# Attention with top-4 expert routing on one core: transposes and logits set between the products of a step, and ScalarE's evacuations in another order

## The chip, the cores and the metric

The kernel runs on one core of a Trainium2 chip. The metric is the device time of one execution in microseconds (us), from which the profile shows the span between the first and the last instruction. The engines are TensorE (PE; its weight loads are listed as PEld), VectorE (DVE), ScalarE (ACT), GpSimd (POOL) and SyncE (SP), which issues most transfers.

## The reference

`x` is 4 batches of 1024 rows of 1024; the context is 4 x 1024 x 512. Cut to what matters:

```python
def xattn(teacher_logits, teacher_features, Wq, bq, Wk, bk):
    query = einsum('bnc,dc->bnd', teacher_features, Wq) + bq
    key = einsum('bnc,dc->bnd', teacher_features, Wk) + bk
    attention = softmax(einsum('bnd,bmd->bnm', query, key), axis=-1)
    return einsum('bln,bmn->blm', teacher_logits, attention)

x = x + xattn(layernorm(x), ctx, Wq, bq, Wk, bk)
x = x + ffn(layernorm(x), ...)   # 32 experts, top 4 per row, SwiGLU with limits
```

The ffn computes logits of each row against `gate_w` (32 x 1024), takes the four largest, weighs them by a softmax, and sends each row through its four experts. In the attention the rows of LN1(x) are multiplied by the transposed attention matrix, so both operands have to be transposed to stand with the contracted index on the partitions.

## The kernel before

The kernel has two parts. The first, `attention_and_routing`, computes the attention, the second layernorm (LN2), the routing and a table of the rows for the experts. The second, `experts`, goes through 32 experts and is not touched. The order in each part is written out by hand: every engine has its own program, and semaphores tie them.

A batch has 8 tiles (NT) of 128 rows. A step `s` works on two batches at once: for batch `b1` it makes tile `s` of the attention matrix (energies, exponent, probabilities, transposes) and of the LN1 rows; for batch `b2`, whose attention matrix is complete, it computes the product of tile `s` and its LN2, and, one tile late (`late`, tile `n = s - 1`), transposes the LN2 rows, computes their logits, ranks and destinations. `schedule` runs the first batch alone, then a hardware loop of three rounds, whose body is steps 2 to 7 of one pair of batches and steps 0 and 1 of the next, and then the last batch's products alone. The steps with `s >= 2` and both batches are 18: six in each of three rounds. In the first two rounds, steps 2 to 5 (`CTX_STEPS`) also transpose a quarter of the next context, and step 7 is followed by the projections `queries_and_keys` of the next batch.

An f32 value is kept as two f16 words, high (HI) and low (LO), so a product of 128 x 1024 x 1024 is three passes (`PASSES`) over 8 blocks and two halves of columns: 48 matmuls of 512 columns into `psM` (line 622). Transposes move 8 blocks of 128 x 128 as 32-bit words into one PSUM tile, `psT` (line 587 for rows and probabilities, line 596 for context). `psT` is shared: LN1 rows (`xnh`), probabilities (`ah`), LN2 rows (`xs2`, shown as `xs`) and context (`cx`, shown as `W`) all pass through it, and each has to be evacuated by ScalarE before the next may enter. The logits are 8 matmuls of 32 columns (line 677), the energies two of 512 (line 581), the rank of a tile two small ones (lines 708, 709).

ScalarE in a step: exponent (500), evacuation of the probabilities (505), high part of the LN2 rows (534), high parts of probabilities and LN1 rows (509, 511), evacuation of the LN2 rows (541), of the context (486), of the LN1 rows (515), exponent of the top four logits (550). VectorE in a step: maximum of the energies (762), LN1, scale, low part of the LN2 rows (786), destinations, low parts of probabilities (774) and LN1 rows (777), top four, then the read of the products (839) and LN2 (732 to 737).

Of the kernel before, what the change touches and what calls it, by code (L numbers as in the profile page):

```python
# [6 lines left out]
ACT = mybir.ActivationFunctionType  # L7
# [6 lines left out]
P = 128  # L14
# [40 lines left out]
def guarded(eng, cond, body):  # L55

    if cond is None:
        body()
    else:
        with eng.If(cond):  # L60
            body()
# [68 lines left out]
def attention_and_routing(nc, g):  # L130
# [8 lines left out]
    with ExitStack() as ctx:  # L139
# [153 lines left out]
        def following(bk):  # L293
            return bk[0], bk[1] + 1

        def per(n, bk, offset):

            return bk[0] * n + (bk[1] * n + offset)

        def tile(bk, offset):  # L300
            return per(NT, bk, offset)
# [174 lines left out]
        def _(act):  # L476
# [17 lines left out]
            def step(s, b1, b2, more):  # L494
# [18 lines left out]
                def rows_out(s):  # L513
                    act.wait_ge(s_xT, tile(b1, s + 1))
                    act.activation(XT_w[:, :, s * P:(s + 1) * P], psT[:, :].rearrange("p (k q) -> p k q", q=P),
                                   ACT.Copy).then_inc(s_xTev, 1)

                if b1 is not None:
                    guarded(act, own, exponent)
                    if s >= 1 and b2 is not None:  # L520
                        guarded(act, own, lambda: attention_out(b1, s - 1))
                    elif s >= 1:

                        if s - 1 in CTX_STEPS:
                            context(following(b1), s - 1 - CTX_STEPS[0])
                        rows_out(s - 1)
# [37 lines left out]
        def _(pe):  # L564
# [14 lines left out]
            def energies(m):  # L579
# [2 lines left out]
                                   qk[:, 1, h * HALF:(h + 1) * HALF], start=True, stop=True)  # L582
                op.then_inc(s_E, 1)

            def transpose_words(src, done):
                for k in range(KH):
                    op = pe.transpose(psT[:, k * P:(k + 1) * P], src[:, k * P:(k + 1) * P], ident[:])
                op.then_inc(done, 1)

            def context(bk, pair):  # L590

# [23 lines left out]
                    context((0, 0), pair)  # L615
                queries_and_keys((0, 0))

            def product(out, bk, t, h, blocks):

                for k in blocks:  # L620
                    for n, (a, c) in enumerate(PASSES):
                        op = pe.matmul(out[:, h * HALF:(h + 1) * HALF], XT[:, k, t * P:(t + 1) * P, a],  # L622
                                       AT[:, par(bk), c, k, h * HALF:(h + 1) * HALF].rearrange("p o q -> p (o q)"),
                                       start=k == 0 and n == 0, stop=k == KH - 1 and n == 2)
                return op

            def step(s, b1, b2, more):
                own = more if s < 2 else None
                late = lagged(b2, s, 1)

                def next_energies():
                    if s < NT - 1:
                        pe.wait_ge(s_exp, tile(b1, s + 1))
                        energies(s + 1)

                if b1 is not None and b2 is None:

                    next_energies()

                if b1 is not None and s >= 1:  # L640
                    def attention_in():
                        alone(pe, s_xTev, tile(b1, s), s_past)
                        pe.wait_ge(s_alo, tile(b1, s))
                        transpose_words(ah_w[(s - 1) % 2], s_AT)
                    guarded(pe, own, attention_in)
                if b2 is not None and s == 0:
                    alone(pe, s_xTev, tile(b2, NT), s_past)
                    pe.wait_ge(s_alo, tile(b2, NT))
                    transpose_words(ah_w[(NT - 1) % 2], s_AT)
                if b2 is not None and s < NT:  # L650

                    if b1 is None and s > 2:
                        pe.wait_ge(s_exp, B * NT)
                        pe.wait_ge(s_x2, tile(b2, s - 1))
                    elif s > 0 or not first(b2):
                        pe.wait_ge(s_x2, tile(b2, s))
                    if s == 0:

                        pe.wait_ge(s_ATev, tile(b2, NT - 1))
                    product(product_of(s, b1), b2, s, 0, range(KH))  # L660
                if b2 is not None and s == 0:
                    alone(pe, s_ATev, tile(b2, NT), s_past)
                if late:
                    bt, n = late
                    if b1 is not None and s >= 1:
                        guarded(pe, own, lambda: alone(pe, s_ATev, tile(b1, s), s_past))
                    pe.wait_ge(s_xs2, tile(bt, n + 1))
                    transpose_words(xs2, s_x2T)
                if b2 is not None and s < NT:
                    product(product_of(s, b1), b2, s, 1, range(KH // 2))  # L670
                if late:

                    pe.wait_ge(s_x2Tev, tile(bt, n + 1))
                    if n >= 1 or not first(bt):
                        pe.wait_ge(s_lgev, tile(bt, n))
                    for k in range(KH):
                        op = pe.matmul(psR[:, 0:E], x2T[:, k, :], gateT[:, k, :], start=k == 0, stop=k == KH - 1)
                    op.then_inc(s_lgt, 1)
                if b1 is not None:
                    if b2 is None and s >= 1:  # L680
                        pe.wait_ge(s_ATev, tile(b1, s))
                    if s in CTX_STEPS:
                        guarded(pe, more, lambda: context(following(b1), s - CTX_STEPS[0]))
                if b2 is not None and s < NT:
                    product(product_of(s, b1), b2, s, 1, range(KH // 2, KH)).then_inc(s_xm, 1)
                if b1 is not None:
                    if s in CTX_STEPS:
                        guarded(pe, more, lambda: alone(pe, s_cTev, per(NT // 2, following(b1), s - CTX_STEPS[0] + 1), s_past))

                    def rows_in():  # L690
                        pe.wait_ge(s_xlo, tile(b1, s + 1))
                        transpose_words(xnh_w, s_xT)
                        if b2 is not None:
                            next_energies()
                    guarded(pe, own, rows_in)
                    if s == NT - 1:
                        def next_batch():

                            alone(pe, s_exp, tile(b1, NT), s_past)
                            if b2 is not None:  # L700
                                alone(pe, s_x2, tile(b2, NT), s_past)
                            queries_and_keys(following(b1))
                        guarded(pe, more, next_batch)
                if late:

                    pe.wait_ge(s_mask, tile(bt, n + 1))
                    pe.wait_ge(s_seen, tile(bt, n + 1))
                    pe.matmul(psQ[:, 0:E], before[:], mask[:, n % 2, :], start=True, stop=False)
                    pe.matmul(psQ[:, 0:E], ones[:], seen[:], start=False, stop=True).then_inc(s_rank, 1)

            schedule(pe, step, prepare)

# [537 lines left out]
```

## Time and profile before

| | |
|---|---|
| time, median of 3 runs | 3249.12 us (3247.87 to 3255.22) |
| profiled execution: time, span | 3258.53 us, 3256.7 us |
| mean granted clock of TensorE | 0.974 |
| PE busy | 3115.6 us (96%) |
| DVE busy | 1721.5 us (53%) |
| ACT busy | 1289.4 us (40%) |
| POOL busy | 592.3 us (18%) |

### The profile page before, as it was taken

The page shows a single profiled execution, that of the slowest core. Times are in us where ns is not written, and L with a number is a line of the kernel's source. Part 1 is how long each engine was busy: PE and PEld are TensorE (multiplying, and loading weights), DVE is VectorE, ACT ScalarE, POOL GpSimd, SP SyncE. Part 2 cuts the span into 40 slices and gives each one's busy share as a digit, 9 for nine tenths or more (in the row PEclk, how much of TensorE's full clock was granted, in tenths as well). Part 3 has the DMA queues.
Part 4 walks back from the last instruction along what each step waited for, and adds up shares of the span by engine and source line. Part 5 has one row for each costly group of instructions (what it writes and reads, how often), then busy time and mean ns, then how long its engine had stood idle before and what let it go on. Part 6 is the DMA issues. An engine that isn't in the chain of part 4 may idle for free.

```text
span 3256.7 us, 46843 instructions
## 1 busy us (share of the span) xinstructions
PE 3115.6 (96%) x15456; PEld 1610.8 (49%) x15457; DVE 1721.5 (53%) x2851; ACT 1289.4 (40%) x1299; POOL 592.3 (18%) x502
## 2 busy tenths in 40 slices
PE   6799999995999999999999999999999999999997
PEld 3455555553454554454554454554444554545553
DVE  3576767764554444555444546454455444554432
ACT  3444434422343343444433434353344433443421
POOL 0022333322111111111111111111111111111111
PEclk8899999997999999999999999999999999999998
DMA  4123222244555555566655656665566655555432
GB/s 150 65 104 111 98 104 98 98 161 138 148 166 139 155 148 155 172 172 168 191 148 155 174 142 195 191 174 155 146 171 168 192 148 155 153 163 143 116 59 58
DMA packets 210440, 468.03 MB, mean 144 GB/s; under 512 B 57762, under 2 KB 57762, under 8 KB 210115
## 3 DMA queue, kind: packets, MB, share of 16 engines
q0 software_dynamic: 45856, 152.33, 20.9%
q10 hardware_dynamic: 94576, 225.46, 20.7%
q1 hardware_dynamic: 69938, 89.38, 8.3%
q8 instruction: 36, 0.59, 0.1%
q14 instruction: 34, 0.27, 0.0%
HBM read 354.64 MB, written 112.46 MB: 143 GB/s over the span
## 4 chain that ended last, share of the span: by engine, by line
PE 74%; DMA 1%; issue 0%; ACT 0%; DVE 0%; SPq 0%; POOL 0%; POOLq 0%
PE psG L1166 23%; PE psU L1166 23%; PE psY L1188 23%; PE psX L1172 4%; PE psA L1179 2%; DMA acc<-y,idxs 0%; DMA idxs<-slots 0%; DMA idxg<-slots 0%; DMA xg<-xn_tab,idxg 0%; DVE y L1113 0%; ACT y L1047 0%; ACT xT L1036 0%; SPq L962 0%; POOL acc L1004 0%; SPq L963 0%
## 5 line engine op out<-in xcount | busy, mean ns | idle before, releaser
L1166 PE MATMUL psG<-W,xT 128*128 128x512 f16 x3456 | 771.4, 380 | 2.8 <-ACT xT L1036 2.8
L1188 PE MATMUL psY<-W,aT 128*128 128x512 f16 x3456 | 769.4, 379 | 1.7 <-ACT aT L1040 1.7
L1166 PE MATMUL psU<-W,xT 128*128 128x512 f16 x3456 | 769.4, 379 | 0.0
L1166 PEld LDWEIGHTS psG<-W,xT 128*128 128x128 f16 x3456 | 338.5, 98 | 412.1 <-issue 4.7
L1188 PEld LDWEIGHTS psY<-W,aT 128*128 128x128 f16 x3456 | 338.0, 98 | 377.3 <-ACT aT L1040 1.9
L1166 PEld LDWEIGHTS psU<-W,xT 128*128 128x128 f16 x3456 | 338.2, 98 | 375.6
L123 DVE SCALAR_TENSOR_TENSOR W<-stage,W 128x2048 f16<-128x2048 f32 x192 | 438.5, 2284 | 3.8 <-ACT W L118 3.8
L1113 DVE SCALAR_TENSOR_TENSOR y<-bias,idxs,y 128x1024 f32<-128x1024 f32 x144 | 184.9, 1284 | 456.2 <-ACT y L1047 456.2
L1004 POOL DMA_INDIRECT acc<-y,idxs x144 | 226.3, 1571 | 986.3 <-DVE y L1113 970.9
L118 ACT ACTIVATE W<-stage 128x2048 f16<-128x2048 f32 x192 | 365.8, 1905 | 48.7 <-issue 38.0
L1047 ACT ACTIVATE y<-psY,idxs 128x1024 f32<-128x1024 f32 x144 | 160.3, 1113 | 515.8 <-DMA idxs<-slots 498.9
L999 POOL DMA_INDIRECT xg<-xn_tab,idxg x146 | 155.2, 1063 | 1094.3 <-PE psX L1172 663.3
L622 PE MATMUL psM<-W,XT 128*128 (+1 forms) x1392 | 333.4, 395 | 2.0 <-DVE xr L839 2.0
L1036 ACT ACTIVATE xT<-psX 128x1024 f32<-128x1024 f32 x145 | 148.6, 1025 | 449.4 <-PE psX L1172 449.4
L1121 DVE SCALAR_TENSOR_TENSOR gt<-psG,bias 128x512 f32<-128x512 f32 x144 | 99.5, 691 | 387.6 <-PE psG L1166 367.0
L1083 ACT ACTIVATE sg<-gt 128x512 f32<-128x512 f32 x144 | 91.0, 632 | 454.8 <-DVE gt L1124 454.5
L1132 DVE SCALAR_TENSOR_TENSOR up<-psU,bias 128x512 f32<-128x512 f32 x144 | 99.5, 691 | 304.5 <-PE psU L1166 304.5
L622 PEld LDWEIGHTS psM<-W,XT 128*128 128x128 f16 x1392 | 141.4, 103 | 161.4 <-issue 24.3
L465 POOL DMA_INDIRECT slots<-pack,dest x128 | 169.4, 1324 | 228.7 <-DVE tok L814 197.6
L1172 PE MATMUL psX<-ident,xg 128*128 128x128 f32 x1160 | 151.3, 274 | 20.8 <-DMA xg<-xn_tab,idxg 20.8
L1172 PEld LDWEIGHTS psX<-ident,xg 128*128 128x128 f32 x1160 | 136.5, 142 | 49.4 <-DMA xg<-xn_tab,idxg 21.7
L1142 DVE SCALAR_TENSOR_TENSOR ahl<-av,ahl 128x512 f16<-128x512 f32 x144 | 105.4, 732 | 43.1 <-ACT ahl L1089 39.7
(136 smaller groups left out, 2309.8 us busy)
## 6 DMA issues: line engine op xcount, KB each, us to landing
stage<-in_L_ffn_w_down ACTq DMA_DIRECT2D x62, 1024.0 KB
stage<-in_L_ffn_w_up ACTq DMA_DIRECT2D x61, 1024.0 KB
stage<-in_L_ffn_w_gate ACTq DMA_DIRECT2D x60, 1024.0 KB
stage<-in_x SPq DMA_DIRECT2D x32, 512.0 KB
xr<-in_x SPq DMA_DIRECT2D x32, 512.0 KB
acc<-xr SPq DMA_DIRECT2D x32, 512.0 KB
xn_tab<-x2h SPq DMA_DIRECT2D x32, 512.0 KB
bias<-in_L_ffn_b_down ACTq DMA_DIRECT2D x32, 512.0 KB
```

Of the source, the lines that this page charges most:

```text
L118: act.activation(W[:, par, HI, c * CHUNK:(c + 1) * CHUNK], stage[:, c % RING, :], ACT.Copy, scale=S_W).then_inc(s_whi, 1)
L123: dve.scalar_tensor_tensor(out=W[:, par, LO, c * CHUNK:(c + 1) * CHUNK], in0=stage[:, c % RING, :], scalar=S_W, in1=W[:, par, HI, c * CHUN ...
L465: pool.indirect_dma_start(out=slots[:, :], out_offset=bass.IndirectOffsetOnAxis(dest[:, n % 2, k:k + 1], 0), in_=pack[:, n % 2, k, :], in_ ...
L622: op = pe.matmul(out[:, h * HALF:(h + 1) * HALF], XT[:, k, t * P:(t + 1) * P, a], AT[:, par(bk), c, k, h * HALF:(h + 1) * HALF].rearrange( ...
L999: pool.indirect_dma_start(out=xg[:], out_offset=None, in_=xn_tab[:, :], in_offset=bass.IndirectOffsetOnAxis(idxg[:, 0:1].bitcast(U32), 0)) ...
L1004: pool.indirect_dma_start(out=acc[:, :], out_offset=bass.IndirectOffsetOnAxis(idxs[:, 0:1].bitcast(U32), 0), in_=y[:], in_offset=None, com ...
L1036: act.activation(xT[:].rearrange("p k q a -> p (k q a)").bitcast(F32), psX[:], ACT.Copy).then_inc(s_xTev, 1)
L1047: act.activation(y[:], psY[:], ACT.Copy, scale=idxs[:, 2:3].bitcast(F32)).then_inc(s_y0, 1)
L1113: dve.scalar_tensor_tensor(out=y[:], in0=bias[:, par, 2 * I:], scalar=idxs[:, 1:2].bitcast(F32), in1=y[:], op0=ALU.mult, op1=ALU.add).then ...
L1166: op = pe.matmul(ps[:], xT[:, k, :, a], weights(par, c, offset + k * I, I), start=k == 0 and n == 0, stop=k == KH - 1 and n == 2)
L1172: op = pe.transpose(psX[:, n * P:(n + 1) * P], xg_w[:, n * P:(n + 1) * P], ident[:])
L1188: op = pe.matmul(psY[:, h * HALF:(h + 1) * HALF], aT[:, k, :, a], weights(par, c, 2 * KH * I + k * H + h * HALF, HALF), start=k == 0 and n ...
```

## The change

For the 18 steps with both batches and `s >= 2`, TensorE runs a new function `both` and ScalarE a new order. The other steps are as before.

On TensorE the eight transposes of the LN2 rows stand one by one before products 6 to 13 of the first half, the eight logits one by one before the first eight products of the second half, and the eight transposes of the probabilities, which stood at the start of the step, one by one before products 4 to 11 of the last twelve. The energies of the next tile follow the products directly, the transposes of the LN1 rows come behind them. On ScalarE the high part of the LN2 rows and their evacuation come right behind the exponent, and the evacuation of the probabilities goes from second place to the place before that of the LN1 rows.

```diff
@@ ScalarE, in step @@
+                if s >= 2 and b1 is not None and b2 is not None:
+                    bt, n = late
+                    exponent()
+                    act.wait_ge(s_xnout[n % 2], per(8 * NT, bt, 16 * (n // 2 + 1)))
+                    act.wait_ge(s_xs2, tile(bt, n + 1))
+                    act.activation(x2h[:, n % 2, :, HI], xs2[:], ACT.Copy, scale=S_ROWS).then_inc(s_hi2, 1)
+                    act.wait_ge(s_x2T, tile(bt, n + 1))
+                    act.activation(x2T[:], psT[:, :].rearrange("p (k q) -> p k q", q=P), ACT.Copy).then_inc(s_x2Tev, 1)
+                    hi_parts()
+                    if s in CTX_STEPS:
+                        guarded(act, more, lambda: context(following(b1), s - CTX_STEPS[0]))
+                    act.wait_ge(s_nv0, tile(bt, n + 1))
+                    act.activation(ex[:, n % 2, :], v8[:, n % 2, 0:TOPK], ACT.Exp, bias=nv0[:, n % 2:n % 2 + 1],
+                                   accum_out=es[:, n % 2:n % 2 + 1]).then_inc(s_ex, 1)
+                    attention_out(b1, s - 1)
+                    rows_out(s)
+                    return
@@ TensorE @@
-            def product(out, bk, t, h, blocks):
+            def product(out, bk, t, h, blocks, beside=None):
 
                 for k in blocks:
                     for n, (a, c) in enumerate(PASSES):
+                        if beside is not None:
+                            beside(3 * (k - blocks[0]) + n)
                         op = pe.matmul(out[:, h * HALF:(h + 1) * HALF], XT[:, k, t * P:(t + 1) * P, a],
...
+            def both(s, b1, b2, more):
+                bt, n = b2, s - 1
+
+                def x2_beside(m):
+                    if m == 6:
+                        alone(pe, s_xTev, tile(b1, s), s_past)
+                        pe.wait_ge(s_xs2, tile(bt, n + 1))
+                    if 6 <= m < 6 + KH:
+                        transpose_block(xs2, s_x2T, m - 6)
+
+                def logits_beside(m):
+                    if m == 0:
+                        pe.wait_ge(s_x2Tev, tile(bt, n + 1))
+                        pe.wait_ge(s_lgev, tile(bt, n))
+                    if m < KH:
+                        logits_block(m)
+
+                def probs_beside(m):
+                    if m == 4:
+                        if s in CTX_STEPS:
+                            guarded(pe, more, lambda: alone(pe, s_cTev, per(NT // 2, following(b1), s - CTX_STEPS[0] + 1), s_past))
+                        pe.wait_ge(s_alo, tile(b1, s))
+                    if m >= 4:
+                        transpose_block(ah_w[(s - 1) % 2], s_AT, m - 4)
+
+                pe.wait_ge(s_x2, tile(b2, s))
+                product(psM, b2, s, 0, range(KH), x2_beside)
+                product(psM, b2, s, 1, range(KH // 2), logits_beside)
+                if s in CTX_STEPS:
+                    guarded(pe, more, lambda: context(following(b1), s - CTX_STEPS[0]))
+                product(psM, b2, s, 1, range(KH // 2, KH), probs_beside).then_inc(s_xm, 1)
+                if s < NT - 1:
+                    pe.wait_ge(s_exp, tile(b1, s + 1))
+                    energies(s + 1)
+                pe.wait_ge(s_ATev, tile(b1, s))
+                pe.wait_ge(s_xlo, tile(b1, s + 1))
+                transpose_words(xnh_w, s_xT)
+                if s == NT - 1:
+                    def next_batch():
+
+                        alone(pe, s_exp, tile(b1, NT), s_past)
+                        alone(pe, s_x2, tile(b2, NT), s_past)
+                        queries_and_keys(following(b1))
+                    guarded(pe, more, next_batch)
+                rank(bt, n)
```

TensorE in step 3 of the loop before, from the transposes of the probabilities on; the context's branch stands before its transposes:

```order
L587 MATMUL psT<-ident,ah 128x128 [waits ln1T_evacuated,prob_lo]
L587 MATMUL psT<-ident,ah 128x128 x7
L656 REGISTER_ALU
L622 MATMUL psM<-W,XT 128x512 [waits x2_ready]
L622 MATMUL psM<-W,XT 128x512 x23
L587 MATMUL psT<-ident,xs 128x128 [waits probT_evacuated,ln2_ready]
L587 MATMUL psT<-ident,xs 128x128 x7
L622 MATMUL psM<-W,XT 128x512 x12
L677 MATMUL psR<-gateT,x2T 128x32 [waits logits_read,ln2T_evacuated]
L677 MATMUL psR<-gateT,x2T 128x32 x7
```

The same step of the changed kernel, its start and then its last part behind the context (the rows of products and inserts in turn go on where the dots stand):

```order
L650 MATMUL psM<-W,XT 128x512 [waits x2_ready]
L650 MATMUL psM<-W,XT 128x512 x5
L603 MATMUL psT<-ident,xs 128x128 [waits ln1T_evacuated,ln2_ready]
L650 MATMUL psM<-W,XT 128x512
L603 MATMUL psT<-ident,xs 128x128
...
L60 UNCONDITIONAL_BRANCH [waits ctxT_evacuated]
L603 MATMUL psT<-ident,ah 128x128 [waits prob_lo]
L650 MATMUL psM<-W,XT 128x512
L603 MATMUL psT<-ident,ah 128x128
...
L598 MATMUL psE<-stage 128x512 [waits exp_done]
L603 MATMUL psT<-ident,xnh 128x128 [waits ln1_lo,probT_evacuated]
```

Runs of eight have become single matmuls with a product behind each; the wait for the context's evacuation now stands within the products, and that for the probabilities' evacuation behind the energies.

ScalarE in the same step, before:

```order
L500 ACTIVATE stage,psm<-psE,nmx 128x1024 [waits negmax_ready]
L505 ISA [waits prob_transposed]
L505 ACTIVATE W<-psT 128x16x128
...
L534 ACTIVATE x2h<-xs 128x1024 [waits ln2_ready]
L509 ACTIVATE ah<-stage,sc 128x1024 [waits prob_scale_ready]
L511 ACTIVATE xnh<-stage 128x1024 [waits ln1_ready]
L541 ACTIVATE x2T<-psT 128x1024 [waits ln2_transposed]
```

and of the changed kernel:

```order
L500 ACTIVATE stage,psm<-psE,nmx 128x1024 [waits negmax_ready]
...
L523 ACTIVATE x2h<-xs 128x1024 [waits ln2_ready]
L525 ACTIVATE x2T<-psT 128x1024 [waits ln2_transposed]
L509 ACTIVATE ah<-stage,sc 128x1024 [waits prob_scale_ready]
L511 ACTIVATE xnh<-stage 128x1024 [waits ln1_ready]
...
L505 ISA [waits prob_transposed]
L505 ACTIVATE W<-psT 128x16x128
```

The evacuation of the probabilities (505) has gone from the second place to the end, and that of the LN2 rows (541, now 525) has come ahead of the high parts of probabilities and LN1 rows.

## Rows read from the trace of the kernel before

**Rows 1.** The page: chain that ended last, and a group of weight loads

```profile
PE 74%; DMA 1%; issue 0%; ACT 0%; DVE 0%; SPq 0%; POOL 0%; POOLq 0%
...
L622 PEld LDWEIGHTS psM<-W,XT 128*128 128x128 f16 x1392 | 141.4, 103 | 161.4 <-issue 24.3
```

**Rows 2.** Stretches between reads of products; us, busy, PEclk, DMA share, GB/s

```profile
174.71:195.77 21.06, 19.77 (x105) 11.41 (x104) 15.14 (x47) 9.92 (x11) 6.36 (x6) 0.92 0.28 101
...
257.10:277.20 20.10, 18.95 (x98) 10.57 (x97) 15.11 (x47) 8.88 (x10) 7.87 (x7) 0.92 0.42 141
...
348.89:373.77 24.88, 20.46 (x103) 12.11 (x102) 15.31 (x48) 10.10 (x11) 8.94 (x9) 0.86 0.25 88
...
526.77:550.58 23.81, 19.30 (x95) 11.13 (x93) 15.53 (x47) 9.07 (x10) 8.91 (x9) 0.86 0.27 92
...
609.85:628.57 18.72, 17.04 (x96) 9.96 (x95) 15.02 (x47) 8.87 (x10) 6.93 (x7) 1.00 0.24 85
...
sum 369.53, PE 340.86 PEld 199.39 DVE 271.87 ACT 168.81 POOL 124.71; mean PE 18.94 PEld 11.08 DVE 15.10 ACT 9.38 POOL 6.93
```

**Rows 3.** Timeline of TensorE in a context step; start, us, idle before

```profile
383.05 1.06 PE L587 MATMUL psT<-ident,xs 128*128 128x128 f32 x8 [0.28 <-ACT W L505]
...
387.61 2.22 PE L677 MATMUL psR<-gateT,x2T 128*128 128x32 f32 x16 [0.90 <-ACT x2T L541]
389.64 1.95 PE L596 MATMUL psT<-ident,W 128*128 128x128 f32 x8
391.38 3.36 PE L622 MATMUL psM<-W,XT 128*128 x12
394.57 1.04 PE L587 MATMUL psT<-ident,xnh 128*128 128x128 f32 x8
395.44 1.88 PE L581 MATMUL psE<-stage 128*128 128x512 f32 x4
397.16 0.30 PE L708 MATMUL psQ<-mask,before 128*128 128x32 f32 x2
...
397.53 1.07 PE L587 MATMUL psT<-ident,ah 128*128 128x128 f32 x8
```

**Rows 4.** Timeline of TensorE in a step 0, without waits

```profile
322.97 2.75 PE L622 MATMUL psM<-W,XT 128*128 x12
325.56 1.87 PE L677 MATMUL psR<-gateT,x2T 128*128 128x32 f32 x16
327.26 2.75 PE L622 MATMUL psM<-W,XT 128*128 x12
```

**Rows 5.** Timeline of VectorE in the step from 609.85 to 628.57

```profile
609.85 1.21 DVE L839 SCALAR_TENSOR_TENSOR xr<-psM,xr 128x1024 f32<-128x1024 f32 x1
...
614.57 1.22 DVE L762 TENSOR_REDUCE mx<-psE 128x1 f32<-128x1024 f32 x1
...
620.26 1.41 DVE L786 SCALAR_TENSOR_TENSOR x2h<-xs,x2h 128x1024 f16<-128x1024 f32 x1 [0.77 <-ACT x2h L534]
...
623.89 1.41 DVE L774 SCALAR_TENSOR_TENSOR ah<-stage,sc,ah 128x1024 f16<-128x1024 f32 x1 [0.23 <-DVE tok L814]
...
628.57 1.21 DVE L839 SCALAR_TENSOR_TENSOR xr<-psM,xr 128x1024 f32<-128x1024 f32 x1
```

**Rows 6.** Timeline of ScalarE in the same step

```profile
617.12 1.87 ACT L505 ACTIVATE W<-psT 128x2048 f16 x1
618.87 1.35 ACT L534 ACTIVATE x2h<-xs 128x1024 f16<-128x1024 f32 x1
```

**Rows 7.** Timeline: context transposes at full clock, and their evacuation

```profile
370.07 1.07 PE L596 MATMUL psT<-ident,W 128*128 128x128 f32 x8
...
371.18 1.02 ACT L486 ACTIVATE W<-psT 128x1024 f32<-128x1024 f32 x1 [4.18 <-PE psT L596]
```

**Rows 8.** Timeline of TensorE at the loop's top

```profile
356.17 1.65 PE L587 MATMUL psT<-ident,ah 128*128 128x128 f32 x7 [2.56 <-issue]
```

**Rows 9.** Timeline of TensorE behind the loop, one batch left

```profile
664.65 5.36 PE L622 MATMUL psM<-W,XT 128*128 x24 [1.14 <-DVE xr L839]
```

More of the change, by code:

```diff
@@ L583, in energies, with transpose_block, logits_block @@
                 op.then_inc(s_E, 1)
+            def transpose_block(src, done, k):
+                op = pe.transpose(psT[:, k * P:(k + 1) * P], src[:, k * P:(k + 1) * P], ident[:])
+                if k == KH - 1:
+                    op.then_inc(done, 1)
             def transpose_words(src, done):
                 for k in range(KH):
-                    op = pe.transpose(psT[:, k * P:(k + 1) * P], src[:, k * P:(k + 1) * P], ident[:])
-                op.then_inc(done, 1)
+                    transpose_block(src, done, k)
+            def logits_block(k):
+                op = pe.matmul(psR[:, 0:E], x2T[:, k, :], gateT[:, k, :], start=k == 0, stop=k == KH - 1)
+                if k == KH - 1:
+                    op.then_inc(s_lgt, 1)
             def context(bk, pair):
@@ L627, in step, with rank @@
+            def rank(bt, n):
+                pe.wait_ge(s_mask, tile(bt, n + 1))
+                pe.wait_ge(s_seen, tile(bt, n + 1))
+                pe.matmul(psQ[:, 0:E], before[:], mask[:, n % 2, :], start=True, stop=False)
+                pe.matmul(psQ[:, 0:E], ones[:], seen[:], start=False, stop=True).then_inc(s_rank, 1)
             def step(s, b1, b2, more):
+                if s >= 2 and b1 is not None and b2 is not None:
+                    both(s, b1, b2, more)
+                    return
@@ L676, in step @@
                     for k in range(KH):
-                        op = pe.matmul(psR[:, 0:E], x2T[:, k, :], gateT[:, k, :], start=k == 0, stop=k == KH - 1)
-                    op.then_inc(s_lgt, 1)
+                        logits_block(k)
                 if b1 is not None:
@@ L704, in step @@
                 if late:
[L706 to L709, printed above, removed]
+                    rank(bt, n)
             schedule(pe, step, prepare)
```

## The prediction

> **What bounds the kernel now.** I read the page first. The chain that ended last is TensorE in the expert part, and the change doesn't touch it [rows 1]. All that can change is the stretch in which two batches overlap, 18 steps of the attention. The view by stretches, cut where VectorE starts its read of the products (line 839), gives 369.5 us for the 18 [rows 2]. Three kinds are seen there: a step that also transposes context (21.06 us), one that doesn't (20.10 us, or 18.72 us at a granted clock of 1.00), and the two at the loop's top (24.88 and 23.81 us). In 13 of the 18 the mean granted clock is 0.92 or, at the loop's top, 0.86; in five it is 1.00. With the two levels of 2.4 and 1.2 GHz, 0.92 over 21 us means 3.4 us at the half clock, so some 1.7 us lost.
>
> The timeline of TensorE shows where the time goes [rows 3]. It waits 0.28 us for ScalarE's evacuation of the probabilities (line 505) and 0.90 us for that of the LN2 rows (line 541). Then come 2.0 us of logits, matmuls of 32 columns, and right after them the next group runs slow: the eight context transposes take 1.74 us and twelve products 3.19 us start to start, where a warm stretch needs 0.87 us for eight transposes and 2.59 us for twelve products [rows 3, 4]. So the clock falls behind the wait and the thin logits.
>
> Then I looked at VectorE, which the busy shares don't suggest. In the warm step from 609.85 to 628.57 it starts both reads of the products with no wait in front, so it is VectorE that sets the 18.72 us [rows 5]. From the read to the next maximum (line 762) it needs 4.72 us, and from the maximum to the next read 14.00 us, of which 0.77 us is a wait for ScalarE's high part of the LN2 rows. ScalarE is late with that because the evacuation of the probabilities (1.87 us) stands in front [rows 6].
>
> **The change, part by part.** I count from the start of the maximum, t = 0. The LN2 rows are then just ready.
>
> *ScalarE's order.* Behind the exponent the next operation starts at 2.55 (617.12 - 614.57). That is now the LN2 high part in place of the probabilities: it starts 1.75 us earlier, ends at 3.9, and VectorE's 0.77 us wait is gone. VectorE's loop becomes 4.72 + 13.23 = 17.95 us. The evacuation of the transposed LN2 rows follows at 3.8 to 4.8 (1.02 us, as long as that of the context from the same tile, [rows 7]); the high part of the probabilities comes later than the LN2 rows but ends by 6.4, before VectorE asks for it at 8.55 (623.89 - 614.57 - 0.77, [rows 5]). The probabilities' evacuation moves to the end of the step.
>
> *Transposes and logits between products.* Does an insert cost less than in a run of its own? Twelve products and the first matmul of what follows are 2.59 us apart, 0.216 us a product, with nothing lost at the join; eight transposes take 0.87 us up to the next group, 0.109 us each; sixteen logits passes 1.70 us [rows 3, 4]. Joins are simply additive, so I take inserts at the same price: gain 0, loss 0. The bounds are 0.05 us a transpose saved if its load hides under a product, and 0.10 us lost per insert if the product's own load is laid bare (the load's mean of 103 ns, [rows 1]).
>
> *TensorE's step.* The work warm is 48 x 0.216 = 10.36, three groups of transposes 2.61, logits 1.70, energies 1.72 and rank 0.37 (395.44 to 397.16 to 397.53): 16.8 us, or 17.6 with context. The dependence that matters runs from VectorE: LN2 rows ready at 0.1 (the six products ahead are done by then), then 18 products and 8 transposes (3.88 + 0.87) to 4.9. The logits' wait, 0.90 us before, ends then as well (4.8), so it falls to about 0.1. Then 12 products and logits (4.29) to 9.2.
> Without context: 12 products and 8 transposes (3.46) end at 12.7. The low part of the probabilities is ready at 9.96, before the first of these transposes at 10.1. VectorE reads at 13.23, so VectorE sets the step: 17.95 us.
> With context: 0.87 more, and a wait that was hidden before. The probabilities' transposes reuse psT, so they wait for the context's evacuation. It ends 2.13 us after the context transposes began (370.07 to 372.20), while TensorE is there after 0.87 + 0.86 us [rows 7]: 0.4 to 0.5 us bare. Products end at 14.0, and the step is 14.0 + 4.72 + 0.1 = 18.8 us, set by TensorE and VectorE in a ring.
> *Behind the products.* TensorE now waits for the evacuation of the probabilities before the LN1 transposes; the energies (1.72) stand ahead of that wait and cover all but 0.3 us of it (1.87 after the last transpose, and a hand-over), and they cover the read of psM (1.21 us) too. Queued behind it are the LN1 transposes (0.87), rank (0.37), six products (1.3): about 4.6 us after the products' end, while the LN2 rows come 4.8 us after VectorE's read. ScalarE's evacuation of the LN1 rows, for which the first LN2 transpose also waits, needs 1.0 us from the end of their transposes and lies beside rank and the six products (1.7). So a wait of 0.2 to 1.0 us will stand at the first LN2 transpose. It costs nothing: VectorE is already what is late.
> *Batch changes.* Twice the projection of the next batch follows. It then waits for evacuation and transposes, 2.0 + 0.87 = 2.9 us behind the products, against 0.87 and the read (2.1 us) before. I charge 0.8 us twice, 1.6 us.
> *Loop's top.* TensorE stands for 2.56 us with no releaser in the profile there [rows 8], and goes on cold. The change leaves this. I keep the 24.88 and 23.81 us and add 0.5 for the context wait.
>
> **Sum.** Seven context steps x 18.8 = 131.6; nine others x 17.95 = 161.6; the loop tops 49.2; batch changes 1.6: 344.0 us against 369.5. The gain is 25.5 us, and it passes to the end, since everything behind waits for the attention. The profiled execution took 3258.5 us (span 3256.7), which would become 3233; the median of the runs is 3249.1, so I forecast **3224**. A measurement here tells about 0.2% (6.5 us) from no change.
>
> **The rivals.**
> *The clock goes on falling.* If products between the logits do not hold the clock up, eleven ordinary steps keep a loss of 1.7 us on TensorE, of which 0.5 us hides behind VectorE in the six without context: 5 x 1.7 + 6 x 1.2 = 15.7 us are given back, 3240. For it: the new wait at the LN2 transposes, with the last transposes and the rank before it. Against it: after a wait of 1.14 us behind the rank the products came at full speed (24 of them in 5.36 us, [rows 9]). 0.18 with all partial cases, 3232 to 3245.
> *VectorE gains nothing.* If another wait takes the place of the 0.77 us, the nine steps stay at 18.7 and the gain is 18 us: 3231. It is inside my main case.
> *Slower: weight loads laid bare.* If switching between fp32 and f16 matmuls leaves a product's load uncovered, each of 24 inserts costs up to 0.1 us, 18 x 24 x 0.1 = 43 us, less 6 us of slack in steps without context: net +12 us, 3261. It decides from 0.07 us per insert, where 18 x 24 x 0.07 minus the slack eats the 25 us. Against it: the additive joins of [rows 3, 4], of which each step has nine. For it: no row shows single inserts. 0.08.
> The Trainium skill states this more sharply (TensorE: Matmul & The Clock Gate, The mechanism): a weight load overlaps a running matmul only if the row groups differ, and all of these use the whole array. By that rule every insert would bring bare loads and the result would be the slower one just worked out, or worse. The trace disagrees already in plain runs: a product with a load of 103 ns follows the last after 216 ns, not after more than 300.
> *No change.* Gains and a persistent low clock cancel, or the loop is held by something that neither engine's rows show. 0.07.
> *More than forecast.* Inserts hide their loads, or the stall at the loop's top shrinks, up to 12 us more: 3212. 0.07.
>
> **How the numbers follow.** Main case 0.60, 3216 to 3232. The range 3212 to 3242 takes in the clock rival. Faster 0.60 + 0.18 + 0.07 = 0.85, same 0.07, slower 0.08.
>
> **What would show it.** Steps of 18.0 us without context and 18.8 us with it from read to read; granted clock 1.00 outside the loop tops; the wait for ScalarE before VectorE's line 786 gone; the logits' wait near 0.1 us; a new TensorE wait of up to 1 us at the LN2 transposes on line 737's result. I am wrong if eight inserted transposes with eight products span clearly more than 2.6 us, or if the clock column still reads 0.92.

## The result and the profile after

The changed kernel takes 3231.59 us (median of 4 runs, 3231.12 to 3233.73) against 3250.76 us for the kernel before (median of 4): a ratio of 0.9938, 95% interval 0.9924 to 0.9952, so 0.5 to 0.8% faster. The forecast was 3224, range 3212 to 3242. The profiled execution went from 3258.53 to 3231.47 us, by 27 us, while the medians are 19 us apart; the last part of the section on the prediction comes back to this.

The views of after in the order in which before was read. First the stretches between VectorE's reads of the products (columns as in [rows 2]):

```profile
191.47:209.94 18.47, 17.69 (x105) 11.49 (x104) 14.99 (x46) 10.37 (x12) 7.18 (x8) 1.00 0.33 116
...
246.90:264.74 17.84, 17.39 (x99) 10.96 (x98) 14.91 (x46) 10.03 (x11) 6.82 (x6) 1.00 0.38 130
...
336.10:360.87 24.77, 19.76 (x101) 12.33 (x100) 15.21 (x48) 8.65 (x13) 9.19 (x9) 0.86 0.26 88
...
503.83:526.84 23.01, 18.59 (x94) 11.53 (x93) 15.13 (x47) 7.72 (x12) 8.74 (x9) 0.85 0.28 95
...
sum 337.90, PE 311.49 PEld 199.15 DVE 269.59 ACT 172.40 POOL 124.19; mean PE 17.31 PEld 11.06 DVE 14.98 ACT 9.58 POOL 6.90
```

The sum of the 18 steps has fallen from 369.53 [rows 2] to 337.90 us, by 31.6 us. A context step takes 18.47, one without 17.84, and the granted clock is 1.00 in all steps except the two at the loop's top, which are hardly shorter than before.

TensorE's timeline of a context step (start, us, idle before and its releaser):

```profile
196.34 0.33 PE L603 MATMUL psT<-ident,xs 128*128 128x128 f32 x1 [0.23 <-DVE xs L816]
196.51 0.38 PE L650 MATMUL psM<-W,XT 128*128 x1
196.72 0.27 PE L603 MATMUL psT<-ident,xs 128*128 128x128 f32 x1
196.83 0.38 PE L650 MATMUL psM<-W,XT 128*128 x1
...
201.30 0.38 PE L650 MATMUL psM<-W,XT 128*128 x1
201.51 0.30 PE L612 MATMUL psR<-gateT,x2T 128*128 128x32 f32 x2
201.66 0.38 PE L650 MATMUL psM<-W,XT 128*128 x1
...
205.75 1.03 PE L650 MATMUL psM<-W,XT 128*128 x4
207.12 0.30 PE L603 MATMUL psT<-ident,ah 128*128 128x128 f32 x1 [0.34 <-ACT W L486]
...
209.75 1.88 PE L598 MATMUL psE<-stage 128*128 128x512 f32 x4
211.76 1.09 PE L603 MATMUL psT<-ident,xnh 128*128 128x128 f32 x8
```

The 0.90 us in front of the logits [rows 3] is gone. In its place stand small waits: 0.23 us for the LN2 rows, 0.34 us for the context's evacuation, and a gap of some 0.3 us between the energies and the LN1 transposes (four passes of 0.43 us from 209.75 on, then 211.76). From 196.51 on, a product takes 0.21 us to the next insert and an insert 0.11 us to its product; a product and a logit together take 0.36 us (201.30 to 201.66).

VectorE's timeline in a step without context, which answers to [rows 5]:

```profile
438.90 1.22 DVE L841 TENSOR_REDUCE mx<-psE 128x1 f32<-128x1024 f32 x1
...
443.70 1.38 DVE L865 SCALAR_TENSOR_TENSOR x2h<-xs,x2h 128x1024 f16<-128x1024 f32 x1
...
451.92 1.21 DVE L918 SCALAR_TENSOR_TENSOR xr<-psM,xr 128x1024 f32<-128x1024 f32 x1
```

The low part of the LN2 rows has no wait in front any more, and from the maximum to the next read it is 13.02 us, where it was 14.00.

Last, what comes behind step 7. The wait of TensorE behind the last products, and the stretches from the read of step 7 to that of step 0:

```profile
281.38 0.38 PE L650 MATMUL psM<-W,XT 128*128 x1
283.68 1.66 PE L603 MATMUL psT<-ident,xnh 128*128 128x128 f32 x8 [1.92 <-ACT W L505]
285.14 8.19 PE L631 MATMUL psM<-W,WT 128*128 128x512 f32 x16
293.16 7.03 PE L631 MATMUL psE<-W,WT 128*128 128x512 f32 x16
```

```profile
282.46:317.27 34.81, 32.74 (x130) 17.57 (x131) 18.17 (x51) 9.73 (x9) 7.15 (x7) 0.95 0.18 62
451.92:485.02 33.10, 31.05 (x130) 16.60 (x131) 18.16 (x51) 9.68 (x9) 7.13 (x7) 1.00 0.19 65
616.43:636.70 20.27, 18.52 (x95) 11.54 (x95) 8.61 (x37) 6.66 (x7) 6.51 (x8) 0.83 0.23 80
```

and the same stretches of the kernel before:

```profile
297.32:330.06 32.74, 31.07 (x130) 16.38 (x129) 18.17 (x51) 8.93 (x10) 6.06 (x5) 1.00 0.19 65
475.38:507.95 32.57, 31.06 (x130) 16.36 (x129) 18.16 (x50) 8.94 (x10) 6.04 (x5) 1.00 0.18 66
647.20:663.37 16.17, 15.33 (x94) 9.57 (x92) 8.74 (x36) 5.88 (x8) 6.50 (x8) 1.00 0.28 99
```

Here 2.07, 0.53 and 4.10 us are given back, 6.7 us in all. Step 7 has no energies, so nothing covers the evacuation of the probabilities: 1.92 us bare in each round. In the first round the first sixteen matmuls of the projections then take 8.0 us in place of 6.9, and the clock of the stretch is 0.95; in the third it is 0.83. In the second round the clock stays at 1.00 behind the same 1.92 us, and only 0.53 us are lost. The account of the profiled executions closes: 31.6 - 6.7, and 1.7 us because the first read of the 18 steps came at 172.98 and not 174.71, and 0.3 us behind 636.70, make the 27 us. The 1.7 us lie in front of the changed steps, and so aren't a gain of the change: the same read lies between 173.5 and 175.1 us in the profiles of the experiments.

### The profile page after: what moved, and what is told of

Read it like the earlier page. It is cut to its first block, busy times and chain, and to the rows that moved or that the text cites. A ratio compares the mean times of both kernels' runs of the same rounds, so it can differ in the third digit from the quotient of the medians.

```text
span 3229.7 us, 46840 instructions
## 1 busy us (share of the span) xinstructions
PE 3088.9 (96%) x15456; PEld 1612.5 (50%) x15457; DVE 1719.9 (53%) x2851; ACT 1294.6 (40%) x1299; POOL 594.1 (18%) x502
## 4 chain that ended last, share of the span: by engine, by line
PE 75%; DMA 1%; issue 0%; ACT 0%; DVE 0%; SPq 0%; POOL 0%; POOLq 0%
PE psG L1245 23%; PE psU L1245 23%; PE psY L1267 23%; PE psX L1251 4%; PE psA L1258 2%; DMA acc<-y,idxs 0%; DMA idxs<-slots 0%; DMA xg<-xn_tab,idxg 0%; DMA idxg<-slots 0%; DVE y L1192 0%; ACT y L1126 0%; ACT xT L1115 0%; SPq L1041 0%; POOL acc L1083 0%; SPq L1042 0%
## 5 line engine op out<-in xcount | busy, mean ns | idle before, releaser
L1245 PEld LDWEIGHTS psG<-W,xT 128*128 128x128 f16 x3456 | 338.5, 98 | 412.6 <-issue 5.2
L650 PE MATMUL psM<-W,XT 128*128 (+1 forms) x1392 | 369.9, 384 | 10.8 <-issue 9.1
L650 PEld LDWEIGHTS psM<-W,XT 128*128 128x128 f16 x1392 | 149.3, 110 | 131.2 <-issue 16.0
L1251 PE MATMUL psX<-ident,xg 128*128 128x128 f32 x1160 | 151.3, 274 | 20.1 <-DMA xg<-xn_tab,idxg 20.1
```

The lines of the kernel that those rows point to most:

```text
L1245: op = pe.matmul(ps[:], xT[:, k, :, a], weights(par, c, offset + k * I, I), start=k == 0 and n == 0, stop=k == KH - 1 and n == 2)
L1251: op = pe.transpose(psX[:, n * P:(n + 1) * P], xg_w[:, n * P:(n + 1) * P], ident[:])
```

## Experiments

Two questions: what holds TensorE's clock up now, and which engine sets a step. Ratios are against the kernel before, run beside them; its median was 3253.3 us for the first four, 3251.9 for the next two, 3255.2 for the last three.

**e1_before_again.** The kernel before, unchanged, for one more profile.

> The kernel before, profiled once more, to see how much of it varies between executions. If the times of before spread because the granted clock falls in other steps each time, the 18 steps with two batches again show some 13 with a granted clock under 1.00, but not the same ones, and their sum lies within some 6 us of 369.5. If the spread comes from the start or from the experts, the same steps are slow and the sum is the same to 1 us.

3257.11 us. The 18 steps sum to 369.65 us, and they are the same steps that are slow: 13 with a clock of 0.92 or 0.86, and 1.00 where it was 1.00. A step that kept its clock, and TensorE's wait in front of its logits in the first profile of before, where that step is 237.75 to 257.10:

```profile
237.29:256.65 19.36, 18.16 (x106) 11.06 (x105) 15.11 (x46) 9.95 (x11) 5.77 (x5) 1.00 0.31 110
```

```profile
251.60 1.97 PE L677 MATMUL psR<-gateT,x2T 128*128 128x32 f32 x16 [0.91 <-ACT x2T L541]
```

So the drops are not chance in these two profiles. But the wait alone doesn't decide on them: it is as long (0.86 to 0.92 us) in the five steps that keep a clock of 1.00. The runs of before beside this one lie between 3247.9 and 3257.3 us, and their mean granted clocks go with it: 0.977 in the three from 3247.9 to 3249.8 us, and 0.974 in the two of 3257.2 and 3257.3. So executions of the same kernel differ in how long the half clock lasts.

**e2_runs.** The inserts put together again at their places; order and waits stay.

```diff
                 def x2_beside(m):
                     if m == 6:
...
-                    if 6 <= m < 6 + KH:
-                        transpose_block(xs2, s_x2T, m - 6)
+                        transpose_words(xs2, s_x2T)
...
                         pe.wait_ge(s_lgev, tile(bt, n))
-                    if m < KH:
-                        logits_block(m)
+                        for k in range(KH):
+                            logits_block(k)
...
                         pe.wait_ge(s_alo, tile(b1, s))
-                    if m >= 4:
-                        transpose_block(ah_w[(s - 1) % 2], s_AT, m - 4)
+                        transpose_words(ah_w[(s - 1) % 2], s_AT)
```

> The changed kernel with each group of eight (LN2 transposes, logits, probabilities' transposes) in one run at the place where its first insert stood; all waits and ScalarE's order as in the changed kernel. Theory A, the new order holds the clock and the inserts as such bring only the logits' 0.07 us each (0.143 in place of 0.213): context steps +0.56 us to 19.0, the others unchanged at 17.8, all clocks 1.00, 7 x 0.56 = 4 us slower than the changed kernel, about 3236. Theory B, the products between the logits hold the clock: with the logits in a run it falls again to 0.92 in most steps, +1.5 us in ten or more of them, 3245 or more.

3232.08 us, ratio 0.9935 (0.9921 to 0.9948): the same as the changed kernel. A context step, one without, the stretch behind the last step 7 and TensorE's wait in it:

```profile
213.20:232.25 19.05, 18.05 (x105) 11.05 (x104) 15.02 (x46) 10.30 (x12) 7.05 (x7) 1.00 0.32 112
422.03:439.88 17.85, 17.19 (x97) 10.23 (x96) 14.91 (x47) 8.64 (x11) 6.29 (x6) 1.00 0.33 119
...
621.81:639.04 17.23, 15.49 (x94) 9.78 (x94) 8.72 (x36) 6.32 (x7) 6.53 (x8) 1.00 0.27 94
```

```profile
622.71 1.09 PE L603 MATMUL psT<-ident,xnh 128*128 128x128 f32 x8 [1.03 <-ACT W L505]
```

Theory A. The context step is 0.58 us longer, eight times 0.07, the other is unchanged, and of the 18 only those at the loop's top have lost their clock (two steps 1, which have the old order, did: 20.20 us at 0.92). The interleaving, the headline of the change, brings 0.07 us for each logit in seven steps, 4.0 us, and nothing that the total shows. It missed the forecast of 3236 for a reason that the stretches behind step 7 show: they take 32.80, 32.81 and 17.23 us, 5.3 us less than in the changed kernel. The run of the probabilities' transposes ends earlier than the single ones, the wait behind the last products of step 7 is 1.03 or 1.04 us in place of 1.92, and the clock stays at 1.00 in all three rounds. So most of what is lost behind step 7 comes with the interleaving of the probabilities.

**e3_hi_second.** In `step` of ScalarE, the high part of the LN2 rows and their evacuation change places.

```diff
+                    act.wait_ge(s_x2T, tile(bt, n + 1))
+                    act.activation(x2T[:], psT[:, :].rearrange("p (k q) -> p k q", q=P), ACT.Copy).then_inc(s_x2Tev, 1)
                     act.wait_ge(s_xnout[n % 2], per(8 * NT, bt, 16 * (n // 2 + 1)))
                     act.wait_ge(s_xs2, tile(bt, n + 1))
                     act.activation(x2h[:, n % 2, :, HI], xs2[:], ACT.Copy, scale=S_ROWS).then_inc(s_hi2, 1)
-                    act.wait_ge(s_x2T, tile(bt, n + 1))
-                    act.activation(x2T[:], psT[:, :].rearrange("p (k q) -> p k q", q=P), ACT.Copy).then_inc(s_x2Tev, 1)
```

> The changed kernel with ScalarE's high part of the LN2 rows behind their evacuation instead of ahead of it, so it is ready about 1.5 us later and VectorE waits some 0.5 to 0.8 us for it. Theory: VectorE sets the steps without context, so these go from 17.85 to 18.3 to 18.6 us, while context steps, set by TensorE behind the LN2 rows, stay at 18.48 or grow by 0.1 to 0.2 only; total +5 to +8 us over the changed kernel, 3237 to 3240. Rival: TensorE sets both kinds; then nothing changes, or it gets faster since the logits' evacuation comes earlier: 3230 to 3232.

3235.14 us, ratio 0.9945 (0.9931 to 0.9959). A context step and one without:

```profile
397.72:416.19 18.47, 17.69 (x105) 11.52 (x104) 15.07 (x46) 10.34 (x12) 7.24 (x6) 1.00 0.33 115
416.19:434.34 18.15, 17.70 (x99) 11.08 (x98) 15.05 (x47) 10.19 (x11) 6.88 (x7) 1.00 0.32 117
```

The step with context has not moved by 0.01 us, that without is 0.3 us longer. So VectorE sets the steps without context and TensorE those with it. The size was less than expected, since VectorE waits only 0.16 to 0.20 us in front of its line 865, which starts 5.08 us behind the maximum in place of 4.83. The total is no better proof, as a drop in a step 1 (20.20 us at 0.92) is in it too.

**e4_step7_as_before.** Step 7 in the old order on both engines.

```diff
-                if s >= 2 and b1 is not None and b2 is not None:
+                if 2 <= s < NT - 1 and b1 is not None and b2 is not None:
```

> The changed kernel with step 7 in the order of before on TensorE and ScalarE; steps 2 to 6 changed. Theory: the new order is wrong for step 7, which has no energies to cover the evacuation of the probabilities: a bare wait of 1.92 us, and behind it a low clock in two of three rounds. From the read of step 7 to that of step 0 the rounds go back from 34.8, 33.1, 20.3 to 32.7, 32.6, 16.2 us, 6.7 us in all, while step 7 itself goes from 17.7 to 18.7 (or 20.1 with a low clock), 3 to 7 us: 0 to 4 us faster than the changed kernel, 3228 to 3232. Rival: the loss belongs to the end of the loop and its code, not to the order: then the 6.7 us stay and step 7 gets slower, 3235 or more.

3229.84 us, ratio 0.9927 (0.9913 to 0.9940). Step 7 of the first round, step 7 of the third, and what follows it:

```profile
266.36:285.02 18.66, 16.91 (x100) 10.14 (x99) 14.98 (x47) 9.58 (x9) 6.94 (x7) 1.00 0.59 221
599.13:619.24 20.11, 18.35 (x97) 10.34 (x96) 15.03 (x48) 9.60 (x9) 7.98 (x8) 0.92 0.23 80
619.24:635.32 16.08, 15.24 (x94) 9.52 (x93) 8.71 (x36) 5.82 (x8) 5.43 (x6) 1.00 0.29 100
```

The stretches behind step 7 are 32.57, 32.56 and 16.08 us, as before the change: the loss comes from what the change does in step 7, and not from the loop's end. Step 7 itself pays 0.9, 0.9 and 2.4 us of it back.

**e5_probs_run.** The probabilities' transposes in one run, two products later.

```diff
-                    if m == 4:
+                    if m == 6:
...
-                    if m >= 4:
-                        transpose_block(ah_w[(s - 1) % 2], s_AT, m - 4)
+                        transpose_words(ah_w[(s - 1) % 2], s_AT)
```

> The changed kernel with the probabilities' eight transposes in one run before the seventh of the last twelve products, not one by one from the fifth on. Their evacuation then starts 1.3 us ahead of the products' end, and the wait for the context's evacuation (0.34 us) has two more products in front. Theory: inserts cost the same in a run, so context steps lose the 0.34 us wait, 18.48 to about 18.15; the others stay at 17.8, bound by VectorE; behind step 7 the bare wait of 1.92 us falls to about 0.6 and the clock holds: 2.4 + 2 to 5 us, some 3225 to 3228. Rival: if single inserts are cheaper than a run, steps with context get slower, 3233 or more.

3223.61 us, ratio 0.9916 (0.9903 to 0.9930). A context step, the read behind the last step 7, and TensorE around the run:

```profile
210.55:228.59 18.04, 17.39 (x105) 11.36 (x104) 15.02 (x47) 10.26 (x12) 6.98 (x7) 1.00 0.34 119
...
612.02:629.26 17.24, 15.49 (x94) 9.81 (x95) 8.69 (x37) 6.32 (x7) 6.52 (x8) 1.00 0.27 94
```

```profile
206.78 1.46 PE L650 MATMUL psM<-W,XT 128*128 x6
208.15 1.07 PE L603 MATMUL psT<-ident,ah 128*128 128x128 f32 x8
209.05 1.46 PE L650 MATMUL psM<-W,XT 128*128 x6
```

In context steps it is as forecast: the evacuation of the context is over when the run begins, and they take 18.04 to 18.11 us. Behind step 7 the result came, but not by the forecast way. 20.27 us become 17.24 with the clock at 1.00, as in e2 (17.23), yet the bare wait has fallen only to 1.59 to 1.62 us, not to 0.6: ScalarE does the exponent of the top four logits first, and begins the evacuation at 281.17 us in the first round, 1.1 us after the run of transposes has given way to products (280.10). In all six stretches of e2 and e5 the clock holds; with a wait of 1.92 us it fell in two of three in the changed kernel and in two of three in e3. A run in the right place is worth more than inserts in a late one.

**e6_hi_first_alone.** The kernel before; only ScalarE's one operation for the high part of the LN2 rows (and its two waits) moves ahead of the evacuation of the probabilities, in the 18 steps.

```diff
+                early = s >= 2 and b1 is not None and b2 is not None
...
                 if b1 is not None:
                     guarded(act, own, exponent)
+                    if early:
+                        late_hi()
                     if s >= 1 and b2 is not None:
                         guarded(act, own, lambda: attention_out(b1, s - 1))
```

> The kernel before, TensorE's order untouched; only ScalarE does the high part of the LN2 rows ahead of the evacuation of the probabilities in the 18 steps. VectorE's wait of 0.77 us goes; TensorE's wait at the LN2 transposes grows from 0.28 to some 1.5 us, and that before the logits falls from 0.90 to near 0, since the LN2 rows' evacuation stays where it was: net +0.4 us on TensorE per step. Theory A, the clock falls because a wait of 0.9 us stands directly before the thin logits: with that wait moved in front of twelve products the clock holds in most steps, each 1.2 us faster, 3230 to 3240. Theory B, the thin logits and the context alone let it fall: clocks stay at 0.92 and the time is 3250 to 3258.

3237.40 us, ratio 0.9954 (0.9940 to 0.9967). A context step, the loop's top, and a step without context:

```profile
212.51:231.88 19.37, 17.89 (x106) 11.13 (x105) 15.12 (x46) 9.88 (x11) 6.96 (x6) 1.00 0.33 110
340.95:365.77 24.82, 20.01 (x105) 12.25 (x104) 15.26 (x46) 10.04 (x11) 7.89 (x7) 0.86 0.27 89
572.27:590.73 18.46, 16.99 (x98) 10.24 (x97) 14.90 (x46) 8.86 (x10) 7.10 (x6) 1.00 0.34 115
```

and TensorE's timeline in the first of them:

```profile
222.99 1.06 PE L595 MATMUL psT<-ident,xs 128*128 128x128 f32 x8 [1.48 <-ACT W L505]
223.89 2.75 PE L630 MATMUL psM<-W,XT 128*128 x12
226.48 1.87 PE L685 MATMUL psR<-gateT,x2T 128*128 128x32 f32 x16
228.18 1.07 PE L604 MATMUL psT<-ident,W 128*128 128x128 f32 x8
229.09 2.75 PE L630 MATMUL psM<-W,XT 128*128 x12
```

Theory A. TensorE waits longer than before in all (1.48 us against 0.28 and 0.90), yet the clock is 1.00 in every one of the 16 steps off the loop's top, and the 18 steps take 349.7 us in place of 369.5. The thin logits with the context behind them are still there, in a row. What has gone is a wait directly in front of them. VectorE's wait of 0.77 us has gone as well, so not all of the 19.8 us is the clock's. With TensorE's program untouched, this one operation gives 0.46% of the 0.62% that the whole change gives.

**e7_hi_first_all, e8_unrolled, e9_unrolled_hi_first_all.** On top of e5: the same operation moved in steps 0 and 1 too; the loop written out; both. The edit of e7 (shortened), and that of e8 (with `guarded` taking True and False):

```diff
+                early = b1 is not None and b2 is not None
...
                     guarded(act, own, exponent)
+                    if early and late:
+                        late_hi()
```

```diff
-            with eng.Fori(0, B - 1) as b:
+            for b in range(B - 1):
                 more = b < B - 2
```

> The kernel with the probabilities' transposes in a run, and ScalarE's high part of the LN2 rows right behind the exponent in steps 0 and 1 with two batches too. Theory, from the moved operation alone: VectorE's wait of 0.77 us in these steps goes and the wait before the logits falls to near 0, so step 1 goes from 18.8 (20.2 where the clock falls) to 18.0 to 18.5 us and never shows 0.92; some 2 to 4 us faster than with the run alone, 3220 to 3222. Rival: in steps 0 and 1 the wait at the LN2 transposes that this creates lets the clock fall there instead; 20.2 stays and the time is 3223 to 3227.

> The kernel with the probabilities' transposes in a run, and the loop of three rounds written out three times, so that no engine jumps back; all work and order are the same, the conditions on the round become constants. Theory: the 24.5 and 21 to 23 us of step 2 at the loop's top are the jump back (instructions that have to be fetched, 4.5 us in which TensorE stands, and the low clock behind it); written out, step 2 takes 18.0 to 18.4 us in all rounds: 9 to 11 us faster, 3213 to 3216. Rival: the stall is that of a batch change or of the address arithmetic of the first step, and stays: 3222 to 3227; or code three times as long makes fetches of its own and is slower.

> Both of the last two edits together. If each does what it does alone, the gains add up: 3210 to 3214. If the gain of the one came from the clock that the other also holds up, it is only as fast as the better of the two.

3219.81 us (0.9895, 0.9879 to 0.9912), 3212.85 us (0.9875, 0.9858 to 0.9891) and 3211.03 us (0.9868, 0.9852 to 0.9885). Of e8, the former loop's top in rounds two and three, with the step 1 ahead of the latter; then that step 1 in e9:

```profile
334.62:352.74 18.12, 17.39 (x104) 11.33 (x103) 15.00 (x47) 10.05 (x13) 6.00 (x5) 1.00 0.33 117
475.37:495.57 20.20, 18.93 (x98) 10.71 (x97) 15.08 (x46) 8.93 (x10) 7.91 (x7) 0.92 0.29 105
495.57:513.31 17.74, 17.01 (x98) 10.69 (x97) 14.89 (x46) 8.64 (x12) 5.86 (x5) 1.00 0.34 119
```

```profile
473.92:492.45 18.53, 17.00 (x98) 10.22 (x97) 15.16 (x47) 8.89 (x10) 6.45 (x7) 1.00 0.33 115
```

The tops take 18.12 and 17.74 us, where e5 had 24.52 and 21.21: the stall belongs to the loop and is gone with it, all of it, with the low clock behind. Writing the loop out also makes constants of the conditions and addresses, so e8 alone doesn't part them from the jump; but steps 3 to 7 in the loop have such conditions and addresses too, and don't stand. Step 1, which still has the old order, keeps the wait in front of the logits in e8 and loses the clock in both rounds that have one (20.14 and 20.20 us); with the operation moved it takes 18.53. In e7 the two steps 1 take 18.53 and 18.54 us too, and the top of the second round 22.70 us at 0.92. The gains of e7 and e8 add up to 3209, and e9 has 3211, which is about the sum. It is 1.3% faster than the kernel before and, by the two ratios, 0.7% faster than the changed one.

## Why the prediction was right, and where it was off

**The steps.** Seven context steps were forecast at 131.6 us and took 129.4; the nine others at 161.6, and took 160.8; the tops at 49.2, and took 47.8. Two readings carried this: that VectorE is what comes next (18.72 us with a wait of 0.77 in it) and that the context's evacuation, hidden before, would stand bare. For that 0.4 to 0.5 us were forecast from start to start. The four products from 205.75 on end their turn at 206.61 and the first transpose starts at 207.12: 0.51 us, of which the profile shows 0.34 as idle. e3 confirms who sets which step.

**The price of an insert.** Joins are additive, I argued, gain 0, loss 0. For transposes that is exact: a product and an insert together take 0.32 us (196.51 to 196.83), which is 0.216 and 0.109. A logit between products costs 0.14 (0.36 less 0.216), not 0.213. Why it costs less was not tested. This term was mis-sized by 0.56 us a step, which is why context steps took less than 18.8 us; e2, with the logits in a run, takes 0.58 us more. The slower rival falls with it: no load was laid bare. A product of the whole array follows an fp32 transpose after 0.11 us, though its own load is recorded with 0.10 us and the transpose's with 0.14. The Trainium skill's rule that loads overlap only between different row groups (TensorE: Matmul & The Clock Gate, The mechanism) disagrees with these rows; that the same section lets a load into the background weight buffer run ahead would fit them.

**The clock.** The reading of [rows 3], that it falls behind the wait and the thin logits, was right, but the prediction left open what would cure it, and named products between the logits as what might hold it. e2 takes these away and the clock stays; e6 takes the wait from in front of the logits, leaves TensorE's program, and the clock comes back in every step off the loop's top. So, off the loop's top and the end of step 7, the clock fell in these profiles only where the wait of 0.9 us stood directly ahead of low activity, and the cure was one ScalarE operation. The wait is needed for the drop and doesn't force it: five of before's 18 steps have it and keep 1.00. What decides between them stays open. The price of the drop was put a little high: context steps take 21.0 us with it and 19.4 without, the others 20.1 against 18.6 to 19.0. Five and six of them make 16 of the 31.6 us by which the 18 steps got shorter.

**Behind step 7.** This is the term that failed. I charged 0.8 us twice for the batch changes and nothing for the third round, 1.6 us where it was 6.7. I had the bare 2 us in the working (2.9 us behind the products) and costed it as a delay. As a delay it was about right, 0.53 us in the round that kept its clock. I did not ask of this new wait what I had asked of the old one: what it does to the clock. And the third round, with no projections behind, was missed: 4.1 us.

**Luck in the sum.** The terms for the steps add up to 342.4 us and measured 337.9, 4.5 us less; behind step 7 it was 5.1 us more than charged. The two misses cancel, and so 24.9 us (31.6 less 6.7) stand against the 25.5 of the working.

**Profile and median.** The sum was made against the profiled execution and then taken off the median. The working gave 25.5 us, the profiled executions differ by 27.0 (1.7 of it in front of the changed steps), the medians by 19.2. Before's median beside the experiments, 3251.9 to 3255.2 us, would make it 20 to 24. The profiled times of before (3258.5, 3257.1) lie at the upper end of its runs, and that of after does not. Both profiled executions of before have a mean granted clock of 0.974, while the runs of before from 3247.9 to 3249.8 us have 0.977 or 0.978. An estimate from this: 0.003 of 3250 us is 9.8 us, and these runs lie 7 to 11 us under the profiled ones. So the profile showed an execution of before with more time at the half clock than most have, and a sum made on it was too large for the median: 24.9 us against 19.2. A plausible reading is that in the faster executions some of the 13 drops do not occur; in which steps stays open.

## What to carry to other kernels

Look for a wait that stands directly in front of low-activity work on TensorE: its price is not its length alone (0.90 us) but also the low clock that can follow (1.3 to 1.6 us a step here), and moving one operation of another engine may cure it without touching TensorE. When an edit leaves a wait bare, check every variant of the step, above all the one that lacks the work that covers it in the others. Before praising an interleaving, run the same order with the inserts in a run: here the order gave all of the gain that the total shows, and the inserts gave 4.0 us in one place and cost 5.3 in another. And when a sum comes out right, compare its terms one by one.

## What the runs showed of the hardware

- At a hardware loop's top TensorE stood for 4.7 us (2.15 and 2.52 us with no releaser, between 338.6 and 343.6 us in the changed kernel). In e5 these steps took 24.5 and 21.2 us, and written out they take 18.1 and 17.7. The Trainium skill names a cause (Runtime: NRT & Kernel Launch, Instruction fetch mechanics): fetching ahead is sequential, and a taken branch to a far target waits for a transfer. The trace agrees: from 338.5 to 343.7 us the two instruction queues carry three transfers, and over the whole program they move 0.49 and 0.20 MB when written out instead of 0.59 and 0.27, in a kernel with more code.
- An fp32 matmul of 32 columns (two passes) costs 0.07 us less between products of 512 columns than in a run; an fp32 transpose of 128 columns costs 0.109 us in either place.
- A wait of 1.48 us ahead of transposes and twelve full products left the clock up in all 16 steps off the loop's top (e6). One of 0.90 us ahead of logits was followed by the half clock in 11 of the 16. Full products behind it are no safeguard for a longer wait: 1.92 us ahead of eight transposes and the projections' matmuls cost the clock in the first round of the changed kernel and not in the second.
